# A graph layer with experts: the mix added on VectorE, fill tables on GpSimd, and 54 constant products on TensorE

## The reference

```
xn = layernorm(x)
h  = xn @ W;  e = exp(-leaky_relu(h@a_l [src] + h@a_r [dst], 0.1))
gnn = elu(segment_sum(e * h[dst], src) / (segment_sum(e, src) + 1e-5))
q  = (xn@w_ql) * (xn@w_qr);  mix = q @ ((xn@w_key).T @ (xn@w_value))
x  = x + gnn + mix
xf = layernorm(x);  p = softmax(max(xf@gate_W + gate_b, 1e-4))       # 8 experts
w  = max(p, 0.1) at the top 2 of p, divided by the sum of these two
out = x + sum over the top 2 of w * (xf @ expert_W[e] + expert_b[e]) / 2
```

## Time and profile before

| | us |
|---|---|
| median of three runs | 1256.27 (1254.42 to 1256.33) |
| the profiled execution | 1256.91 |
| its span in the profile | 1255.1 |
| TensorE busy | 1185.3 (94%) |
| VectorE, ScalarE, GpSimd busy | 760.4, 304.9, 489.1 |

### The profile page before, as it was taken

One profiled execution on the slowest core, in us unless ns is written; L12 is line 12 of the kernel. 1 busy time (PEld: TensorE's weight loads), 2 busy tenths in 40 slices (PEclk: granted clock), 3 DMA queues, 4 the chain that ended last, 5 costly groups with the idle time before them and its releaser, 6 DMA issues.

```text
span 1255.1 us, 16236 instructions
## 1 busy us (share of the span) xinstructions
PE 1185.3 (94%) x5799; PEld 1000.1 (80%) x5799; DVE 760.4 (61%) x1515; ACT 304.9 (24%) x412; POOL 489.1 (39%) x441
## 2 busy tenths in 40 slices
PE   6999999999999999999999999899966899999996
PEld 5788888878788899999977878788855688878884
DVE  8979522453334777767665337989667823553544
ACT  2412112232211111111012323333242400421222
POOL 3960677878785000000000007456412434444443
PEclk9999999999999999999999999999967999999998
DMA  5111442844221323211054422353355965694855
GB/s 206 34 34 34 126 112 68 282 118 104 73 52 30 88 95 99 86 55 55 22 151 141 129 96 75 139 205 137 127 210 195 367 130 93 156 310 89 234 93 125
DMA packets 89623, 156.08 MB, mean 124 GB/s; under 512 B 14628, under 2 KB 45086, under 8 KB 89428
## 3 DMA queue, kind: packets, MB, share of 16 engines
q1 hardware_dynamic: 74148, 129.76, 30.4%
q0 software_dynamic: 15408, 25.44, 11.5%
HBM read 112.95 MB, written 42.04 MB: 123 GB/s over the span
## 4 chain that ended last, share of the span: by engine, by line
PE 53%; POOL 23%; DVE 10%; issue 8%; DMA 4%; ACT 1%; DVEq 1%; SPq 0%; POOLq 0%; ACTq 0%
POOL tab_d L671 17%; PE ps L1579 16%; PE ps L1580 15%; PE ps L1581 15%; POOL in L656 4%; DVE e_lo L1409 2%; DMA e_raw<-in_L_ffn_expert_W 2%; PE ps L1707 2%; PE ps L1750 2%; PE ps L1817 1%; DMA q_in<-in_L_mix_w_query_right 1%; PE ps L1666 1%; DVE place_sum L1120 1%; DVE place L1118 1%; DVE place L1117 1%
## 5 line engine op out<-in xcount | busy, mean ns | idle before, releaser
L671 POOL DMA_INDIRECT tab_d<-val_i,addr_i x160 | 209.6, 1310 | 109.3 <-issue 109.3
L1579 PE MATMUL ps<-e_hi,lt_hi 128*128 128x512 f32 x368 | 147.7, 401 | 14.0 <-DVE yb L1554 8.6
L686 POOL TENSOR_TENSOR att_part<-att 128x640 f32<-128x640 f32 x10 | 17.6, 1760 | 356.5 <-PE ps L1581 348.6
L1581 PE MATMUL ps<-e_hi,lt_lo 128*128 128x512 f32 x368 | 145.0, 394 | 0.0
L1580 PE MATMUL ps<-e_lo,lt_hi 128*128 128x512 f32 x368 | 144.8, 394 | 0.0
L1579 PE MATMUL ps<-xt_hi,q_hi 128*128 128x416 f32 (+1 forms) x384 | 143.0, 372 | 0.0
L1580 PE MATMUL ps<-xt_lo,q_hi 128*128 128x416 f32 (+1 forms) x384 | 136.0, 354 | 0.0
L1581 PE MATMUL ps<-xt_hi,q_lo 128*128 128x416 f32 (+1 forms) x384 | 135.5, 353 | 0.0
L774 POOL DMA_INDIRECT out<-y,row_put x46 | 74.8, 1626 | 98.5 <-DVE y L1559 67.8
L1253 DVE TENSOR_TENSOR cnt<-ps,cnt 128x256 f32 x208 | 87.4, 420 | 38.4 <-PE ps L1707 27.0
L1579 PEld LDWEIGHTS ps<-e_hi,lt_hi 128*128 128x128 f32 x368 | 70.1, 190 | 31.0 <-DVE yb L1554 16.8
(11 more groups left out here) (292 smaller groups left out, 2670.3 us busy)
## 6 DMA issues: line engine op xcount, KB each, us to landing
e_raw<-in_L_ffn_expert_W SPq DMA_DIRECT2D x64, 512.0 KB
acc<-in_x SPq DMA_DIRECT2D x18, 512.0 KB, 9.0
w_raw<-in_L_mix_w_key SPq DMA_DIRECT2D x16, 512.0 KB
h_d<-hs SPq DMA_DIRECT2D x18, 256.0 KB
q_in<-q_d SPq DMA_DIRECT2D x9, 512.0 KB
h_in<-h_d SPq DMA_DIRECT2D x9, 512.0 KB, 5.7
mix_d<-ms SPq DMA_DIRECT2D x18, 256.0 KB
mix_in<-mix_d SPq DMA_DIRECT2D x9, 512.0 KB, 3.2
```

The lines of the kernel that those rows point to most:

```text
L671: nc.gpsimd.indirect_dma_start(out=tab_d, out_offset=bass.IndirectOffsetOnAxis(ap=addr_i[0:EP, j:j + 1], axis=0), in_=val_i[0:EP, j:j + 1] ...
L1579: nc.tensor.matmul(o, lh, rh, start=(k == 0), stop=False)
L1581: return nc.tensor.matmul(o, ll, rh, start=False, stop=(k == last_k))
```

## The change

The mix job's bank is emptied by VectorE: `mix_add` adds the PSUM bank to x, which SP has loaded into `xm`, and SP stores the sum to `mix_d`; the GNN stage loads the sum alone, and GpSimd's addition is gone. The first histogram comes one job later. The bounds are copied as soon as the scan gives them, with a semaphore of their own, for which SP, ScalarE and TensorE wait before their nine register loads; TensorE's stand now ahead of the token products. VectorE loads one register per expert. The row weights are worked out without dividing by the sum of the exponentials first. The fill tables `pad_r`, `pad_c` are made on GpSimd by sixteen operations, one pair per expert. ScalarE scales y. Five instead of six parts of the next expert's weights are split ahead. And TensorE multiplies a constant by a constant (`keep_busy`, 128 x 128, fp32, into a bank that no one reads) 54 times: 2 behind the first transposes after the last GNN product, 2 behind each of three gates, 14 behind the last gate, 14 behind the register loads, and 18 behind the token products.

```diff
-        ms = at("ms", X + HALF, [P, 2, HALF])
+        xm = at("xm", X + HALF, [P, 2, HALF])
...
-        mix_in = at("mix_in", R2 + 2 * D, [P, 2, D])
...
-        last_c = at("last_c", EX + 3 * D, [P, NE, NSLOT], f16)
...
-        phase("MIX", ["act"] * (NH * NT))
+        phase("MIX", ["dve"] * (NH * NT))
...
-        AHEAD = [4] + [6] * (NE - 2)
+        AHEAD = [4] + [5] * (NE - 2)
...
-        TICK_FIRST = 3
+        TICK_FIRST = 4
...
+            def load_residual(j):
+                t, h = divmod(j, NH)
+                if j >= 2:
+                    sp.wait_ge(s_ms[j % 2], 16 * (j // 2))
+                sp.dma_start(xm[0:ROWS[t], j % 2, :], x[t * P:t * P + ROWS[t], h * HALF:(h + 1) * HALF]).then_inc(s_xr[j % 2], 16)
+
             sp.wait_ge(s_full, first["MIX"])
             load_tile(2)
+            for s in s_qs:
+                sp.wait_ge(s, 16 * KB)
+            for j in range(2):
+                load_residual(j)
...
-                    sp.dma_start(mix_d[t * P:t * P + ROWS[t], h * HALF:(h + 1) * HALF], ms[0:ROWS[t], h, :]).then_inc(s_ms[h], 16)
+                    j = NH * t + h
+                    sp.dma_start(mix_d[t * P:t * P + ROWS[t], h * HALF:(h + 1) * HALF], xm[0:ROWS[t], j % 2, :]).then_inc(s_ms[j % 2], 16)
+                    if 1 <= j and j + 1 < NH * NT:
+                        load_residual(j + 1)
...
-                    sp.dma_start(mix_in[0:ROWS[t], t % 2, :], mix_d[t * P:t * P + ROWS[t], :]).then_inc(s_mx[t % 2], 16)
-                    sp.dma_start(x_in[0:ROWS[t], t % 2, :], x[t * P:t * P + ROWS[t], :]).then_inc(s_mx[t % 2], 16)
+                    sp.dma_start(x_in[0:ROWS[t], t % 2, :], mix_d[t * P:t * P + ROWS[t], :]).then_inc(s_mx[t % 2], 16)
...
-            sp.wait_ge(s_route, 1)
+            sp.wait_ge(s_bounds, 1)
...
-                if 1 <= t <= NT:
-
-                    i = t - 1
-                    pool.wait_ge(s_mx[i % 2], 32 * (i // 2 + 1))
-                    v = x_in[0:ROWS[i], i % 2, :]
-                    nc.gpsimd.tensor_tensor(v, v, mix_in[0:ROWS[i], i % 2, :], ALU.add).then_inc(s_xm, 1)
...
-            G.tensor_tensor(pad_t[:, :], pad_ok[:, :], tokv[:, 0:1].to_broadcast([P, NE]), ALU.mult).then_inc(s_padt, 1)
+            step(G.tensor_tensor(pad_t[:, :], pad_ok[:, :], tokv[:, 0:1].to_broadcast([P, NE]), ALU.mult))
+            for e in range(NE):
+                G.tensor_scalar(pad_r[:, e, :], io16[:, :], pad_at[:, e:e + 1], None, ALU.is_equal)
+                last = G.tensor_scalar(pad_c[:, e, :], io16[:, 0:NSLOT], last_b[:, e:e + 1], pad_t[:, e:e + 1], ALU.is_equal, ALU.mult)
+            last.then_inc(s_pad, 1)
...
-                    evac(mix_job(t, h), ms[0:ROWS[t], h, :], rows=ROWS[t])
...
-            act.wait_ge(s_route, 1)
+            act.wait_ge(s_bounds, 1)
...
-                    act.wait_ge(s_mm, i * 3 + 2)
-                    block_hi(i + 1, 0)
-                    act.wait_ge(s_mm, i * 3 + 3)
-                    block_hi(i + 1, 1)
+                    for h in range(NH):
+                        c = slice(h * HALF, (h + 1) * HALF)
+                        act.wait_ge(s_mm, i * 3 + (2 + h))
+                        block_hi(i + 1, h)
+                        act.wait_ge(s_sc[h], i * 16 + 16)
+                        act.wait_ge(s_ye, i * 2 + (3 + h))
+                        act.sem_inc(s_passed, 1)
+                        nc.scalar.activation(y[:, c], yb[:, c], ACT.Copy, scale=w_slot[:, bass.ds(i, 1)]).then_inc(s_sum2, 1)
...
+            def mix_add(j):
+
+                t, h = divmod(j, NH)
+                w, n = ROWS[t], mix_job(t, h)
+                dve.wait_ge(s_xr[j % 2], 16 * (j // 2 + 1))
+                dve.wait_ge(s_full, n + 1)
+                nc.vector.tensor_tensor(xm[0:w, j % 2, :], ps[0:w, n % NB, :], xm[0:w, j % 2, :], ALU.add).then_inc(s_free_dve, 1)
...
+                    if j > 3 * NQ:
+                        mix_add(j - 3 * NQ - 1)
...
+                    mix_add(NH * NT - 1)
...
-                        dve.wait_ge(s_xm, i + 1)
+                        dve.wait_ge(s_mx[i % 2], 16 * (i // 2 + 1))
...
+            V.tensor_copy(bounds[:, 1:NE + 1], g_cum[:, :]).then_inc(s_bounds, 1)
...
-            V.tensor_copy(bounds[:, 1:NE + 1], g_cum[:, :])
+            dve.wait_ge(s_gexp, 1)
+            V.tensor_reduce(g_t[:, :], g_p[:, :, :], AX.X, ALU.add)
...
-            dve.wait_ge(s_gexp, 1)
-            link(V.tensor_reduce(g_t[:, :], g_p[:, :, :], AX.X, ALU.add))
-            link(V.reciprocal(g_t[:, :], g_t[:, :]))
-            link(V.tensor_tensor(g_p[:, :, :], g_p[:, :, :], over_experts(g_t[:, :]), ALU.mult))
-            link(V.tensor_scalar(g_p[:, :, :], g_p[:, :, :], W_THRES, None, ALU.max))
+            both = w12[:, :].rearrange("p (c t) -> p c t", c=2)
             link(V.tensor_tensor(g_prod[:, :, :, :], g_pick[:, :, :, :], g_p[:, :, :].unsqueeze(1).to_broadcast([P, 2, NT, NE]), ALU.mult))
-            link(V.tensor_reduce(w12[:, :].rearrange("p (c t) -> p c t", c=2), g_prod[:, :, :, :], AX.X, ALU.add))
+            link(V.tensor_reduce(both, g_prod[:, :, :, :], AX.X, ALU.add))
+            link(V.scalar_tensor_tensor(both, g_t[:, :].unsqueeze(1).to_broadcast([P, 2, NT]), W_THRES, both, ALU.mult, ALU.max))
             link(V.tensor_tensor(g_t[:, :], w12[:, 0:NT], w12[:, NT:2 * NT], ALU.add))
             link(V.reciprocal(g_t[:, :], g_t[:, :]))
             link(V.scalar_tensor_tensor(g_t[:, :], g_t[:, :], 1.0 / TOPK, valid[:, :], ALU.mult, ALU.mult))
-            for c in range(2):
-                last = V.tensor_tensor(w12[:, c * NT:(c + 1) * NT], w12[:, c * NT:(c + 1) * NT], g_t[:, :], ALU.mult)
-            link(last)
+            link(V.tensor_tensor(both, both, g_t[:, :].unsqueeze(1).to_broadcast([P, 2, NT]), ALU.mult))
...
-            dve.wait_ge(s_padt, 1)
-            V.tensor_tensor(last_c[:, :, :], io16[:, 0:NSLOT].unsqueeze(1).to_broadcast([P, NE, NSLOT]),
-                            last_b[:, :].unsqueeze(2).to_broadcast([P, NE, NSLOT]), ALU.is_equal)
-            link(V.tensor_tensor(pad_r[:, :, :], io16[:, :].unsqueeze(1).to_broadcast([P, NE, P]),
-                                 pad_at[:, :].unsqueeze(2).to_broadcast([P, NE, P]), ALU.is_equal))
-            V.tensor_tensor(pad_c[:, :, :], last_c[:, :, :], pad_t[:, :].unsqueeze(2).to_broadcast([P, NE, NSLOT]), ALU.mult).then_inc(s_pad, 1)
...
-            first_block = [dve.value_load(bounds[0:1, e:e + 1], min_val=0, max_val=NBLK) for e in range(NE + 1)]
+            first_block = [0]
...
+                first_block.append(dve.value_load(bounds[0:1, e + 1:e + 2], min_val=1, max_val=NBLK))
...
-                    dve.wait_ge(s_sum2, i * 2 + 1)
                     for h in range(NH):
                         c = slice(h * HALF, (h + 1) * HALF)
+                        dve.wait_ge(s_sum2, i * 2 + (1 + h))
                         dve.wait_ge(s_mm, i * 3 + (1 + 2 * h))
                         V.tensor_tensor(yb[:, c], ps[:, h, :], bias[:, e % 2, c], ALU.add).then_inc(s_ye, 1)
-                        if h == 0:
-                            block_lo(i + 1, 0)
-                        dve.wait_ge(s_sc[h], i * 16 + 16)
-                        dve.wait_ge(s_ye, i * 2 + (3 + h))
-                        V.tensor_scalar(y[:, c], yb[:, c], w_slot[:, bass.ds(i, 1)], None, ALU.mult).then_inc(s_sum2, 1)
-                        if h == 1:
-                            block_lo(i + 1, 1)
+                        block_lo(i + 1, h)
...
+            SPARE = gnn_sum(NT - 1) % NB
+            assert SPARE in (0, 1, 3)
+            pe.wait_ge(*released(gnn_sum(NT - 1)))
+
+            def keep_busy(times):
+
+                for _ in range(times):
+                    nc.tensor.matmul(ps[:, SPARE, 0:P], ident[:, :], ones[:, :], start=True, stop=True)
+
             rows_transposed(NT - 2)
-            gate(NT - 4)
-            gate(NT - 3)
-            gate(NT - 2)
+            keep_busy(2)
+            for i in range(NT - 4, NT - 1):
+                gate(i)
+                keep_busy(2)
             rows_transposed(NT - 1)
             gate(NT - 1)
+            keep_busy(14)
...
             pe.wait_ge(s_gtot, 1)
             nc.tensor.matmul(ps[:, 7, 0:NE], tri2[:, :], g_tot[:, :], start=True, stop=True)
             nc.tensor.matmul(ps[:, 7, NE:2 * NE], ones[:, :], g_tot[:, :], start=True, stop=True).then_inc(s_gtotp, 1)
 
+            pe.wait_ge(s_bounds, 1)
+            first_block = [pe.value_load(bounds[0:1, e:e + 1], min_val=0, max_val=NBLK) for e in range(NE + 1)]
+            keep_busy(14)
             for c in range(2):
                 pe.wait_ge(s_toks, c + 1)
                 for t in range(NT):
                     last = nc.tensor.matmul(ps[:, 2, 0:NSLOT], tok_r[:, c * NT + t, :], tok_c[:, c * NT + t, :],
                                             start=(t + c == 0), stop=(t == NT - 1 and c == 1))
             last.then_inc(s_tokp, 1)
+            keep_busy(18)
...
+            keep_busy(18)
             pe.wait_ge(s_non, 1)
```

(17 more changed lines are left out.)

## The result

The changed kernel took 1264.28 us (median of 4, 1259.51 to 1264.97) against 1255.5 (median of 4; the 1256.27 above was that of three of them) for the one before: ratio 1.0064, 95% interval 1.0043 to 1.0085. Run again in experiment r1: 1266.59 (11 runs, 1259.70 to 1269.63) against 1258.09 (34 runs, 1251.62 to 1264.43), ratio 1.0050 (1.0028 to 1.0071). So it is slower by 6 to 9 us (8.0 and 6.3 by the ratios, 8.8 and 8.5 by the medians). The forecast was 2 us slower. Its range, 1250.5 to 1267, holds both medians; the forecast proper, D with 1254 to 1262, holds neither.

What follows compares the result with a forecast made beforehand. TensorE works 94% of the span, losing time only where it idles or runs at 1.2 GHz. Terms +2.1 + 0 - 9.4 + 16.7 - 7.4 = +2.0 gave span 1257.1, median 1258.3 us; range 1250.5 to 1267.

Steps and rivals of the forecast that it cites:

- D: Whole kernel: the main forecast, 1254 to 1262 us, chance 0.50.
- Sum: Whole kernel: all stage terms added, +2.0 us, giving a span of 1257.1 and a median of 1258.3.
- query term: Query products, TICK_FIRST 3 to 4: TensorE's waits join into one of about 5.9 us near 420; +2.1 us.
- expert term: Expert blocks: shorter early waits and AHEAD 5 gain, ScalarE's y and extra splits cost; -7.4 us (-12 to -3).
- C: GNN or mix stage: GNN gain stays away or a mix load is late; +5 to +9, 1265 us, chance 0.08.
- B: Routing: a constant pass costs twice a transpose's, or e_lo keeps GpSimd out altogether; about 1267 us, chance 0.15.
- Mix: Mix stage: VectorE's additions replace ScalarE's copies, it has room and loads come in time; 0 (to +1) us.
- GNN: GNN products: without GpSimd's additions a 4.87 us wait and the half clock behind it go; -9.4 us.
- margin of 0.4 us: GNN products: VectorE comes 5.3 us earlier, barely enough to remove TensorE's 4.87 us wait for xg.
- Routing: Gate and routing: constants, register loads and GpSimd's tables delay the first expert block to 968.7; +16.7 us (+8 to +20).
- A: Routing: clock holds or GpSimd's tables run ahead of e_lo, so it costs less; about 1251 us, chance 0.27.
- first expert product before 962: Start of the expert blocks: a sign listed as showing the forecast wrong; it had the first block at 968.7.

Runs made afterwards that it cites:

- r2: Changed kernel with TICK_FIRST back at 3, all else as changed; +2.9 us against the kernel before (0.9998 to 1.0045).
- r5: Kernel before with the mix part alone (VectorE adds the mix to x, GpSimd's addition out); -7.5 us (0.9921 to 0.9956).
- r9: Changed kernel without constants, fill tables on VectorE, TICK_FIRST 3; 1244.40 us against 1257.66 for the kernel before, ratio 0.9881.
- r10: As r9, with TensorE's nine register loads again behind the pad_n product; -9.1 us against the kernel before (0.9889 to 0.9937).
- r11: As r9, with the first 22 constants kept; -10.5 us against the kernel before (0.9888 to 0.9932).
- r3: Changed kernel with all 54 constant products left out; -2.9 us against the kernel before (0.9956 to 0.9996).
- r12: Kernel before with the 54 constants alone, register loads where they were; +6.8 us (1.0030 to 1.0067).
- r4: Changed kernel with the fill tables on VectorE again, GpSimd's sixteen operations out; -0.7 us against the kernel before (0.9969 to 1.0012).
- r6: Changed kernel with VectorE scaling y again; +9.3 us against the kernel before (1.0044 to 1.0087).
- r7: Changed kernel with AHEAD 6 for the later experts again; +10.0 us against the kernel before (1.0044 to 1.0096).
- r8: Changed kernel without the last 14 and 18 constants, first 22 kept; -1.3 us against the kernel before (0.9962 to 1.0004).

## Why the forecast held, and which sizes were off

- **Sum.** Forecast +2.0; by the stages of the first profile +2.6 (-2.0 up to the first mix product, +0.6 -9.3 +16.0 -4.0 +1.4, -0.2 at the end). The medians say +8.5 to +8.8; the first profile is below them because it had the query chunk early. By stages, with the query term at its mean of +2.1: +2.1 + 0.6 - 9.3 + 16.0 - 2.8 = +6.6 by the first profile and +2.1 + 0.6 - 9.3 + 17.5 - 3.3 = +7.6 by r1's. By stages the forecast was about 5 us too low, 4.1 to 4.6 of it in the expert term; the 1 to 2 us between these sums and the medians have no place. That the range held owes much to its width of 16.5 us: both medians lie above D, nearest to the numbers of C (1265) and B (1267), and neither mechanism, a lost GNN gain or a dearer pass, occurred.
- **Query, +2.1 (0 to +3.5).** The size holds: 2.3 us from the chunk's arrival to the first mix product, and 0.6 in the mix stage. The wait moves to the one near 420, but it is seldom 5.9 us: the seven profiles with TICK_FIRST 4 have 0.29, 2.53, 2.60, 2.62, 2.64, 3.78 and 6.68, and in all but the first of these the clock fell to 0.50 in it or behind it. I had taken the chunk's date as fixed. It follows the store `al_d` and was 411.6, 418.3 and 421.1 in three executions, so that one profile says little: -4 to +4 us for single executions.
- **Mix, 0 (to +1).** 0: with TICK_FIRST 3 the stage takes 112.9 us with the mix part (r2, r5, r9, r10, r11) as without it. The 0.6 more in the changed kernel (113.5) come with TICK_FIRST 4, whose last histogram products fall into this stage: they belong to the query term.
- **GNN, -9.4.** -9.3, and r5 alone shows it belongs to the removed addition. The margin of 0.4 us held in all twelve profiles with the mix part: rival C is out. Scores take 2.36 us at most now, where 3.33 was the earlier trace rows.
- **Routing, +16.7.** +16.0 and +17.5 in the two profiles of this kernel; rivals A and B are out. The sum is right, its parts are not, and their errors cancel; that the total fits so well is luck. From the GNN end the totals are 0.7 to 2.3 us later than before, where 3.6 stood. That is not the constants' price: without them (r3, r9) the totals come after 16.6 and 16.7 us, where it was 18.2 before, as the clock fell 5.7 us behind the GNN end instead of 3.9, and the three gates took 6.1 us instead of 7.7; against these the constants cost 2.2 to 3.9, and against the kernel before 2.3 (r12). From the totals the pad_n product is another 9.1 later, where 9.8 stood. The register loads in front cost nothing by themselves: without the late constants this stretch takes 8.9 us with them there (r3, r9), with them behind (r10) and in the kernel before. ScalarE's lt_hi and lt_lo were ready at +6.4, not +10.6 (947.8 in the first profile, 958.4 when moved by the 10.6 us). But GpSimd's tables took 13.3 us and not 6.6 plus about 4: 0.48 us for 29 columns where I had 0.3, and 4.9 us more for three operations beside e_lo. The constants and the tables lie one behind the other on the path, so their costs add: off the 54.7 us of r1, r3 takes 10.4, r4 9.0 and r9 both, 20.4. The sign "first expert product before 962" is not met by 957.39, since it stands 10.6 us later on the prediction's scale.
- **Experts, -7.4 (-12 to -3).** This is the term that was mis-sized: -2.8 to -3.3, with the tail's 0.2. By the starts of the 23 blocks, the first four took 55.6 us and 54.9, against 61.3 before: -5.6 to -6.3 where -7.7 stood. From the fifth block on the forecast had +0.3 and it was +3.1 to +3.3: a block at a change of expert takes 13.4 us where it took 12.5 (three of them; steady blocks 11.8 in both), the last 13.1 instead of 11.6, and only the one that ends at 1111 gained, 0.9 (0.7 in r1) instead of 1.7. r6 and r7 split the 0.9: with y on VectorE it is 12.8, with AHEAD 6 13.2. So ScalarE's y ahead of e_hi costs 0.65 us per change and AHEAD 5 another 0.25, where I had 0.4 for both.
- **The clock.** In all profiles it fell to 0.50 within 8 us of the GNN end, constants or not, and with constants it was back at 1.0 between 922.2 and 925.6 and from 935.9 to 946.1 in the first profile. The Trainium skill (TensorE: Matmul & The Clock Gate, What's actually happening) says that activity lifts the clock; the trace agrees, 0.70 against 0.55 to 0.58 in the mean of the stage. It bought nothing in the routing: what ended the waits was a chain of other engines, and the busy TensorE made it longer. Behind it the early constants may have given back 1 to 3 us (expert products 285.4 against 288.2 in r8 and r3, 288.3 against 289.3 in r11 and r9), single profiles each.
- **The port.** A table operation of 0.60 us becomes 2.52 beside two e_lo of 1.2 us each, and e_lo keeps its 1.2. The Trainium skill (SBUF — State Buffer, Who interferes with whom) has VectorE with two SBUF inputs and a GpSimd instruction that reads SBUF exclude each other for whole instructions; the trace agrees, and here GpSimd is the one that waits.

## What to carry to other kernels

A filler product is free only in a gap that the same engine waits out: ask what stands behind it in program order. Of the 54, the 32 in front of products that others waited for cost 6 to 7 us, and a higher clock did not shorten a stage that other engines set.

Moving work to an idle engine must count who uses SBUF beside it: three VectorE operations of 2.0 us in all (r4: 0.40, 1.22, 0.40) became sixteen of 13.3 on GpSimd. And one profile is one draw: here a single transfer moved the whole by 5 us, which only many runs and a second profile showed. Where an edit hangs on such a date, measure from the date and not from the start of the stage: that took the scatter out of the query term.

## What the runs showed of the hardware that was not expected

- A GpSimd TENSOR_SCALAR on 128 partitions takes 0.60 us with 128 columns and 0.48 with 29: by these two, some 0.44 us does not depend on the columns.
- A constant fp32 product of 128 columns took 0.24 us at full clock (4.26 us for 18), near the 0.22 that the transposes' rows gave.
- Between executions of kernels that are alike up to there (the first profile and r3) ScalarE got the query chunk behind `al_d` at 411.58 and at 421.08 us, 9.5 us apart.
- A store of 5.0 KB in single words, `al_d`, took 10.5 to 12.5 us from issue to landing in the fourteen profiles, and the 512 KB load of the chunk, issued 0.6 to 7.1 us behind it on the same queue, was there only 2.5 to 3.7 us after it had landed.
